# Attention's exponentials: the clip on GpSimd, both heads' sums in one VectorE instruction, six buffers

## The chip, the cores and the metric

The kernel runs on one core of one Trainium2 chip. The metric is the device time of one execution in microseconds (us). Before the change it is 1333.87 us, the median of 3 runs (1332.39 to 1336.94).

## The reference, cut to what matters

A block of a gated cross-attention model in float32: attention of 2048 rows over 1601 context rows, and then a quantised feed-forward network (FFN).

```python
# attention: x (1, 2048, 256), ctx_1024 (1, 1601, 256), 16 heads of 64
q = (lat @ Wq); k, v = split(ctx @ Wkv)
attn = einsum('bhnd,bhsd->bhns', q, k) * D ** (-0.5)
attn = jnp.clip(attn, -11.0, 11.0)
attn = jax.nn.softmax(attn, axis=-1)
out = einsum('bhns,bhsd->bhnd', attn, v)
x = x + tanh(g_xattn[0]) * (out @ Wo + bo)
# FFN: weights quantised to 4 bits by blocks of 32, activations to 16 bits
up = act_qdq(x @ lpbq_dequant(w_up).T); gate = act_qdq(x @ lpbq_dequant(w_gate).T)
...
x = x + tanh(g_ffn[0]) * (o @ lpbq_dequant(w_down).T)
```

The kernel clips the exponentials, not the scores: exp grows with its argument, so clipping exp(s) to exp(-11) and exp(11) gives the same numbers.

## The kernel before, in words

**Segments and tiles.** Attention is 32 segments (`SEGS`, `t0` from 0 to 31): 8 pairs of heads by 4 blocks of 512 query rows. A segment runs over 13 tiles (`ST`, `st` from 0 to 12) of 128 context rows, the last of 65. Each engine has its own program, written out by hand; semaphores order them, and an engine waits at the head of its own queue.

**One tile.** PE makes the scores of both heads (`scores`, L916) in PSUM, two buffers deep. ScalarE takes the exponentials of both heads into a slot of `e_buf` (L443, 128x1024). VectorE clips them in place (L662). PE multiplies them with V (`values`, L932). The softmax denominators are sums over the context, so the clipped tiles are also added into `acc`: head 0 by VectorE (`add_a`, L622), head 1 by GpSimd (L346), 128x512 each. `e_buf` has 4 slots, and an exponential waits until its slot's `values` and both sums are done.

**PE's order.** Within a segment PE runs `scores(st + 2)`, then what `segment_jobs` puts at `st`, then `values(st)`. So between the end of `scores(st)` and the start of `values(st)` lie at least four matmul groups. The jobs are projections of K and V for the next pair at 0, Q and the denominators (`den`) at 4, and the output projection (`y`) at 10. They share two PSUM banks; a bank is free once the engine that takes its result has done so.

**VectorE beside the tiles.** For the segment before, it joins the two halves of the output (`join_out`, L643), inverts the denominators in four pieces at tiles 6 and 7 (L629, from PSUM), scales the output with them at tile 8 (`scale_out`, L637, which the `y` job waits for), and adds `y` to `xacc` at tile 12 (L652).

**Other work.** In segments 25 to 27 the FFN's weights are quantised: maxima, scales and rounding on VectorE (L559, L599, L600, L604), two products a weight piece on GpSimd (L360, 128x768), two pieces a segment. In segments 30 and 31 VectorE also does the FFN's layer norm of finished rows (`ffn_norm`, L531 to L559). In segment 0 GpSimd adds the output bias to `xacc` (L351). GpSimd scales Wo with the gate once in four segments (L332). DMA issues stand on SP alone.

Of the kernel before, what the change touches and what calls it, by code (L numbers as in the profile page):

```python
# [106 lines left out]
def attention_ffn(nc, x, ctx_rows, g_xattn, g_ffn, ln_l_w, ln_l_b, ln_c_w, ln_c_b,  # L107
                  Wq, Wkv, Wo, bo, w_gate, w_up, w_down, out):
    with ExitStack() as ctx:
# [196 lines left out]
        def _(pool):  # L306
# [17 lines left out]
            def run(seg):  # L324
                t0 = seg.t0
                if t0 % NBS == 0:
                    p = t0 // NBS

                    pool.wait_ge(w_loaded[p % 2], (p // 2 + 1) * 64)
                    if t0 > NBS:  # L330
                        await_job(pool, ("y", t0 - NBS - 1, 1), seg)
                    pool.tensor_tensor(wo_g[:, p % 2, :], wo_raw[:, p % 2, :], tg[:, 0:1].to_broadcast([P, DM]),  # L332
                                       ALU.mult).then_inc(wo_scaled, 1)
                for st in range(1, ST):
                    r = rows_of(st)

                    pool.wait_ge(clip_done, seg.count(ST, st + 1))
                    if st == 1:
                        if t0 >= 2:

                            await_job(pool, ("den", t0 - 2), seg)
                        a = e_buf[:, (ST * t0) % E_BUFS, 1, :]
                    else:
                        pool.wait_ge(sum_b, seg.count(ST - 1, st - 1))
                        a = acc[0:r, t0 % 2, 1, :]
                    pool.tensor_tensor(acc[0:r, t0 % 2, 1, :], a, e_buf[0:r, (ST * t0 + st) % E_BUFS, 1, :],  # L346
                                       ALU.add).then_inc(sum_b, 1)
                    if t0 == 0 and st > ST - 9:

                        for t in range(2 * (st - ST + 8), 2 * (st - ST + 9)):  # L350
                            pool.tensor_tensor(xacc[:, t, :], xacc[:, t, :], bo_t[:, :], ALU.add).then_inc(bias_added, 1)  # L351

                    n, at = divmod(st, 6)
                    if WQ0 <= t0 < WT0 and at in (2, 5) and n < 2:

                        w = 2 * (t0 - WQ0) + (0 if at == 2 else 1)
# [160 lines left out]
        def _(dve):  # L517
# [137 lines left out]
            def run(seg):  # L655
                t0 = seg.t0
                p = t0 // NBS + 1
                for st in range(ST):
# [437 lines left out]
```

## Time and profile before

| | us |
|---|---|
| median of 3 runs (lowest, highest) | 1333.87 (1332.39, 1336.94) |
| the profiled execution | 1334.15 |
| its span | 1332.2 |
| around the span | 1.95 |
| busy: PE, VectorE, GpSimd, ScalarE | 1201.8, 1113.6, 704.4, 602.3 |

The span runs from the first to the last instruction; the profiled execution's own time is that span and what lies around it. Busy time counts an instruction from its start to its end, waits for a port inside it included. Matmuls overlap, so their starts say more than their lengths.

### The profile page before, as it was taken

The page shows a single profiled execution, that of the slowest core. Times are in us where ns is not written, and L with a number is a line of the kernel's source. Part 1 is how long each engine was busy: PE and PEld are TensorE (multiplying, and loading weights), DVE is VectorE, ACT ScalarE, POOL GpSimd, SP SyncE. Part 2 cuts the span into 40 slices and gives each one's busy share as a digit, 9 for nine tenths or more (in the row PEclk, how much of TensorE's full clock was granted, in tenths as well). Part 3 has the DMA queues.
Part 4 walks back from the last instruction along what each step waited for, and adds up shares of the span by engine and source line. Part 5 has one row for each costly group of instructions (what it writes and reads, how often), then busy time and mean ns, then how long its engine had stood idle before and what let it go on. Part 6 is the DMA issues. An engine that isn't in the chain of part 4 may idle for free.

```text
span 1332.2 us, 21513 instructions
## 1 busy us (share of the span) xinstructions
PE 1201.8 (90%) x8427; PEld 501.4 (38%) x8427; DVE 1113.6 (84%) x1432; ACT 602.3 (45%) x682; POOL 704.4 (53%) x457
## 2 busy tenths in 40 slices
PE   4999999999999999999999999999889988699118
PEld 2433333333333333333333333333223322377118
DVE  6598888888888888888888888889999998857985
ACT  2544444444444444444444444444334543158642
POOL 1685655556556555665565556566776655102400
PEclk9999999999999999999999999999999999699559
DMA  4000000000000000000000002000000000000001
GB/s 148 1 1 17 1 1 1 13 5 1 1 2 16 1 1 1 17 1 1 1 17 1 1 1 88 1 1 1 1 1 1 1 1 1 0 1 1 0 0 64
DMA packets 17107, 13.90 MB, mean 10 GB/s; under 512 B 2221, under 2 KB 16750, under 8 KB 17006
## 3 DMA queue, kind: packets, MB, share of 16 engines
q1 hardware_dynamic: 17006, 12.53, 3.0%
q8 instruction: 67, 1.10, 0.3%
q14 instruction: 34, 0.28, 0.1%
HBM read 10.43 MB, written 2.10 MB: 9 GB/s over the span
## 4 chain that ended last, share of the span: by engine, by line
PE 65%; DVE 21%; issue 7%; ACT 5%; POOL 1%; DMA 0%; POOLq 0%; SPq 0%; DVEq 0%
PE ps L932 21%; PE ps L916 20%; DVE e_buf L662 6%; PE ps L1027 6%; PE ps L890 4%; PE ps L847 4%; DVE oT L637 4%; DVE rden L629 4%; PE ps L855 4%; PE ps L864 3%; DVE acc L622 3%; ACT e_buf L443 2%; PE ps L875 2%; ACT z L498 1%; PE ps L836 1%
## 5 line engine op out<-in xcount | busy, mean ns | idle before, releaser
L346 POOL TENSOR_TENSOR acc<-acc,e_buf 128x512 f32<-128x512 f32 (+1 forms) x352 | 583.1, 1657 | 365.1 <-DVE e_buf L662 364.4
L443 ACT ACTIVATE e_buf<-ps 128x1024 f32<-128x1024 f32 (+1 forms) x416 | 426.2, 1025 | 492.3 <-PE ps L916 490.9
L662 DVE TENSOR_SCALAR e_buf<-e_buf 128x1024 f32<-128x1024 f32 (+1 forms) x416 | 472.5, 1136 | 150.4 <-ACT e_buf L443 147.2
L932 PE MATMUL ps<-e_buf,vb 64*64 64x512 f32 (+1 forms) x3328 | 473.5, 601 | 44.0 <-DVE e_buf L662 42.8
L622 DVE TENSOR_TENSOR acc<-acc,e_buf 128x512 f32<-128x512 f32 (+1 forms) x352 | 254.7, 724 | 0.0
L916 PE MATMUL ps<-qb,kb_even 64*64 64x512 f32 (+1 forms) x1664 | 234.6, 595 | 1.3 <-ACT e_buf L443 1.3
L916 PE MATMUL ps<-qb,kb_odd 64*64 64x512 f32 (+1 forms) x1664 | 232.8, 593 | 0.0
L932 PEld LDWEIGHTS ps<-e_buf,vb 64*64 64x64 f32 (+1 forms) x3328 | 118.4, 132 | 301.2 <-issue 191.8
L916 PEld LDWEIGHTS ps<-qb,kb_even 64*64 64x64 f32 (+1 forms) x1664 | 63.5, 131 | 134.3 <-issue 117.2
L916 PEld LDWEIGHTS ps<-qb,kb_odd 64*64 64x64 f32 (+1 forms) x1664 | 63.4, 131 | 132.1 <-issue 114.2
L629 DVE RECIPROCAL rden<-ps 128x128 f32<-128x128 f32 x124 | 109.0, 919 | 0.0
L346 POOL TENSOR_TENSOR acc<-e_buf 128x512 f32<-128x512 f32 x32 | 41.2, 1288 | 69.0 <-DVE e_buf L662 69.0
L1027 PE MATMUL ps<-hT,wgu 128*128 128x512 f32 x288 | 69.6, 404 | 1.8 <-DVE hT L753 1.8
L890 PE MATMUL ps<-wo_g,oT 128*128 128x256 f32 x256 | 66.6, 404 | 2.4 <-issue 2.4
L847 PE MATMUL ps<-latT,wst 128*128 128x512 f32 x128 | 65.2, 632 | 1.1 <-ACT latT L385 1.1
L890 PEld LDWEIGHTS ps<-wo_g,oT 128*128 128x128 f32 x256 | 47.4, 196 | 38.7 <-issue 32.6
L370 POOL TENSOR_SCALAR z<-z 128x1024 uint16<-128x1024 f32 x12 | 14.4, 1200 | 89.5 <-ACT z L500 89.5
L1027 PEld LDWEIGHTS ps<-hT,wgu 128*128 128x128 f32 x288 | 55.2, 193 | 15.6 <-DVE hT L753 2.2
L559 DVE TENSOR_REDUCE fst<-gt 128x2 f32<-128x1024 f32 x36 | 43.5, 1213 | 17.9 <-ACT gt L484 17.9
L637 DVE TENSOR_TENSOR oT<-oT,rden 128x512 f32<-128x512 f32 x31 | 54.8, 1767 | 0.0
L864 PEld LDWEIGHTS ps<-wst,ctxT 128*128 128x128 f32 (+1 forms) x416 | 49.4, 187 | 11.2 <-issue 11.2
L855 PE MATMUL ps<-ctxT,wst 128*128 128x512 f32 (+1 forms) x128 | 52.0, 533 | 0.0
(102 smaller groups left out, 755.4 us busy)
## 6 DMA issues: line engine op xcount, KB each, us to landing
xacc<-in_x_dram SPq DMA_DIRECT2D x4, 512.0 KB, 7.5
wst<-in_L_xattn_Wkv_dram SPq DMA_DIRECT2D x16, 128.0 KB, 2.4
out_dram<-z SPq DMA_DIRECT2D x8, 256.0 KB, 2.2
e_buf<-in_ctx_dram SPq DMA_DIRECT2D x3, 512.0 KB, 4.9
wst<-in_L_xattn_Wq_dram SPq DMA_DIRECT2D x8, 128.0 KB, 2.3
wo_raw<-in_L_xattn_Wo_dram SPq DMA_DIRECT2D x8, 128.0 KB, 3.1
z<-in_L_ffn_w_gate_dram SPq DMA_DIRECT2D x1, 768.0 KB, 5.1
z<-in_L_ffn_w_up_dram SPq DMA_DIRECT2D x1, 768.0 KB, 6.9
```

What stands on the lines that cost most here:

```text
L346: pool.tensor_tensor(acc[0:r, t0 % 2, 1, :], a, e_buf[0:r, (ST * t0 + st) % E_BUFS, 1, :], ALU.add).then_inc(sum_b, 1)
L443: nc.scalar.activation(e_buf[0:r, g % E_BUFS, :, :], sc[0:r, g % 2, :, :], ACT.Exp, scale=float(DH) ** -0.5).then_inc(exp_done, 1)
L622: dve.tensor_tensor(acc[0:r, t0 % 2, 0, :], a, e_buf[0:r, (ST * t0 + st) % E_BUFS, 0, :], ALU.add).then_inc(sum_a, 1)
L629: ins = dve.reciprocal(rden[:, c * w:(c + 1) * w], ps_m[:, bank, c * w:(c + 1) * w])
L637: dve.tensor_tensor(oT[:, t % 2, :], oT[:, t % 2, :], rden[:, :], ALU.mult).then_inc(norm_done, 1)
L662: dve.tensor_scalar(tile, tile, EXP_LO, EXP_HI, ALU.max, ALU.min).then_inc(clip_done, 1)
L847: ins = pe.matmul(bank, wst[:, at[0], 0, k, :], latT[:, k, b * NB:(b + 1) * NB], start=(k == 0), stop=(k == KT - 1))
L855: ins = pe.matmul(bank[:, 0:w], wst[:, at[0], 1, k, :], ctxT[:, k, b * NB:b * NB + w], start=(k == 0), stop=(k == KT - 1))
L890: ins = pe.matmul(bank[:, DM * m:DM * m + DM], oT[:, t % 2, n0:n0 + P], wo_g[:, p % 2, :], start=True, stop=True)
L916: ins = pe.matmul(sc[at:at + n, g % 2, h, :], kb[p % 2][rows, P * st + at:P * st + at + n], qb[rows, t0 % 2, :], start=True, stop=True)
L932: ins = pe.matmul(ps_o[DH * h:DH * h + DH, half, :], vb[rows, p % 2, st, DH * h:DH * h + DH], e_buf[rows, g % E_BUFS, h, :], start=(st == ...
L1027: ins = pe.matmul(out_ap, lhs(i), rhs(j), start=(first and n == 0), stop=(last and n == 2))
```

## The change

GpSimd now clips each tile of exponentials (both heads, in place). VectorE no longer clips; it adds both heads' sums in one 128x1024 instruction (`add_e`), and one semaphore, `summed`, stands for the two. The bias additions (four of 128x1024) and the weight products go to VectorE. `e_buf` has six slots. The product for Wo is issued after the clip of tile 6, not at the segment's head.

```diff
-E_BUFS = 4
+E_BUFS = 6
...
+                for st in range(ST):
+                    tile = e_buf[0:rows_of(st), (ST * t0 + st) % E_BUFS, :, :]
+                    pool.wait_ge(exp_done, seg.count(ST, st + 1))
+                    pool.tensor_scalar(tile, tile, EXP_LO, EXP_HI, ALU.max, ALU.min).then_inc(clip_done, 1)
+                    if st == 6 and t0 % NBS == 0:
+                        p = t0 // NBS
+                        pool.wait_ge(w_loaded[p % 2], (p // 2 + 1) * 64)
...
-                        act.wait_ge(sum_a, back.count(ST - 1, s0))
-                        act.wait_ge(sum_b, back.count(ST - 1, s0))
+                        act.wait_ge(summed, back.count(ST - 1, s0))
...
+            def add_e(seg, st):
 
                 t0, r = seg.t0, rows_of(st)
                 if st == 1:
-                    a = e_buf[:, (ST * t0) % E_BUFS, 0, :]
+                    a = e_buf[:, (ST * t0) % E_BUFS, :, :]
                 else:
-                    a = acc[0:r, t0 % 2, 0, :]
-                    dve.wait_ge(sum_a, seg.count(ST - 1, st - 1))
+                    a = acc[0:r, t0 % 2, :, :]
+                    dve.wait_ge(summed, seg.count(ST - 1, st - 1))
                 dve.wait_ge(clip_done, seg.count(ST, st + 1))
...
+                dve.tensor_tensor(acc[0:r, t0 % 2, :, :], a, e_buf[0:r, (ST * t0 + st) % E_BUFS, :, :],
+                                  ALU.add).then_inc(summed, 1)
...
-                    r, g = rows_of(st), ST * t0 + st
-                    dve.wait_ge(exp_done, seg.count(ST, st + 1))
-                    tile = e_buf[0:r, g % E_BUFS, :, :]
-                    dve.tensor_scalar(tile, tile, EXP_LO, EXP_HI, ALU.max, ALU.min).then_inc(clip_done, 1)
-                    if st >= 2:
-                        add_a(seg, st - 1)
-                    elif st == 0 and t0 >= 1:
-                        add_a(Seg(t0 - 1), ST - 1)
-                    elif st == 1 and t0 >= 1:
+                    if st >= 1:
+                        add_e(seg, st)
+                    elif t0 >= 1:
                         join_out(seg, t0 - 1)
+                    if t0 == 0 and 4 <= st < 4 + NBS:
+                        add_bias(st - 4)
...
-                        if st < 2:
-                            w_scales(w + st)
-                        if st in (7, 11):
-                            w_integers(w + st // 11)
+                        if st in (0, 6):
+                            w_scales(w + st // 6)
+                        if st in (1, 7):
+                            w_multiply(w + st // 7, 2, w_inverse, w_scaled)
+                        if st in (2, 8):
+                            w_integers(w + st // 8)
+                        if st in (3, 9):
+                            w_multiply(w + st // 9, 1, w_round, w_quant)
```

VectorE in an ordinary segment, from the sum at tile 5 to that at tile 8 (L662 is the clip, L622 the sum of head 0, L629 the inversion, L637 the scaling). Before:

```order
L662 TENSOR_SCALAR e_buf<-e_buf 128x1024
L622 TENSOR_TENSOR acc<-acc,e_buf 128x512
L629 RECIPROCAL rden<-ps 128x128 x2
L662 TENSOR_SCALAR e_buf<-e_buf 128x1024
L622 TENSOR_TENSOR acc<-acc,e_buf 128x512
L629 RECIPROCAL rden<-ps 128x128 x2
L662 TENSOR_SCALAR e_buf<-e_buf 128x1024
L622 TENSOR_TENSOR acc<-acc,e_buf 128x512
L637 TENSOR_TENSOR oT<-oT,rden 128x512
L662 TENSOR_SCALAR e_buf<-e_buf 128x1024
L622 TENSOR_TENSOR acc<-acc,e_buf 128x512
```

After, a whole segment's sums up to tile 11 (L604 is the sum of both heads, L618 the inversion, L626 the scaling):

```order
L604 TENSOR_TENSOR acc<-e_buf 128x1024
L604 TENSOR_TENSOR acc<-acc,e_buf 128x1024 x5
L618 RECIPROCAL rden<-ps 128x128 x2
L604 TENSOR_TENSOR acc<-acc,e_buf 128x1024
L618 RECIPROCAL rden<-ps 128x128 x2
L604 TENSOR_TENSOR acc<-acc,e_buf 128x1024
L626 TENSOR_TENSOR oT<-oT,rden 128x512
L604 TENSOR_TENSOR acc<-acc,e_buf 128x1024 x3
```

The clips are gone from between the sums, the inversions and the scaling; the scaling stands behind the sum of tile 8 as before behind that of tile 7.

GpSimd at the start of a segment whose number divides by four (L332 is the product for Wo, L346 the sum of head 1). Before:

```order
L332 TENSOR_TENSOR wo_g<-wo_raw,tg 128x256
L346 TENSOR_TENSOR acc<-e_buf 128x512
L346 TENSOR_TENSOR acc<-acc,e_buf 128x512 x10
L346 TENSOR_TENSOR acc<-acc,e_buf 65x512
L346 TENSOR_TENSOR acc<-e_buf 128x512
L346 TENSOR_TENSOR acc<-acc,e_buf 128x512 x10
```

After (L329 is the clip, L335 the product for Wo):

```order
L329 TENSOR_SCALAR e_buf<-e_buf 128x1024 x7
L335 TENSOR_TENSOR wo_g<-wo_raw,tg 128x256
L329 TENSOR_SCALAR e_buf<-e_buf 128x1024 x5
L329 TENSOR_SCALAR e_buf<-e_buf 65x1024
L329 TENSOR_SCALAR e_buf<-e_buf 128x1024 x12
```

The clips stand one behind another, with nothing between them but that product.

VectorE at tiles 6 to 8 of segment 25, the first with weight work (L604 is the rounding, L622 the sum). Before:

```order
L622 TENSOR_TENSOR acc<-acc,e_buf 128x512
L629 RECIPROCAL rden<-ps 128x128 x2
L662 TENSOR_SCALAR e_buf<-e_buf 128x1024
L622 TENSOR_TENSOR acc<-acc,e_buf 128x512
L629 RECIPROCAL rden<-ps 128x128 x2
L604 TENSOR_SCALAR z<-z 128x768
L662 TENSOR_SCALAR e_buf<-e_buf 128x1024
L622 TENSOR_TENSOR acc<-acc,e_buf 128x512
L637 TENSOR_TENSOR oT<-oT,rden 128x512
```

After (L534, L574, L575 are the scales of the second weight piece, L592 its first product, L604 the sum, L626 the scaling):

```order
L618 RECIPROCAL rden<-ps 128x128 x2
L534 TENSOR_REDUCE wsc<-z 128x24
L574 TENSOR_SCALAR wsc<-wsc 128x24
L575 RECIPROCAL wsc<-wsc 128x24
L604 TENSOR_TENSOR acc<-acc,e_buf 128x1024
L618 RECIPROCAL rden<-ps 128x128 x2
L592 TENSOR_TENSOR z<-z,wsc 128x768
L604 TENSOR_TENSOR acc<-acc,e_buf 128x1024
L626 TENSOR_TENSOR oT<-oT,rden 128x512
```

The scales have come from tile 1 to tile 6, and the product that GpSimd did stands ahead of the sum and the scaling at tile 8.

## Rows read from the trace of the kernel before

**Rows 1.** Page: the span of the profiled execution.

```profile
span 1332.2 us, 21513 instructions
```

**Rows 2.** Windows: stretch, us, busy time of each engine (instructions), PEclk, DMA share, GB/s.

```profile
93.00:420.00 327.00, 319.85 (x2334) 117.68 (x2333) 277.13 (x324) 148.88 (x164) 191.68 (x119) 1.00 0.02 6
...
890.00:1005.00 115.00, 102.92 (x724) 35.96 (x720) 108.23 (x123) 46.10 (x51) 82.07 (x49) 0.97 0.00 1
```

**Rows 3.** Timeline: ScalarE's L429 copies, one a segment: start us, us, instruction.

```profile
384.26 0.59 ACT L429 COPY oT<-ps 128x512 f32<-128x512 f32 x1 [0.80 <-PE ps L932]
...
418.65 0.59 ACT L429 COPY oT<-ps 128x512 f32<-128x512 f32 x1 [0.81 <-PE ps L932]
...
450.37 0.59 ACT L429 COPY oT<-ps 128x512 f32<-128x512 f32 x1 [0.81 <-PE ps L932]
...
889.41 0.59 ACT L429 COPY oT<-ps 128x512 f32<-128x512 f32 x1 [0.80 <-PE ps L932]
...
1004.36 0.59 ACT L429 COPY oT<-ps 128x512 f32<-128x512 f32 x1 [0.81 <-PE ps L932]
...
1067.76 0.59 ACT L429 COPY oT<-ps 128x512 f32<-128x512 f32 x1 [0.81 <-PE ps L932]
...
1104.26 0.59 ACT L429 COPY oT<-ps 128x512 f32<-128x512 f32 x1 [0.81 <-PE ps L932]
...
1145.80 0.59 ACT L429 COPY oT<-ps 128x512 f32<-128x512 f32 x1 [11.33 <-PE ps L932]
```

**Rows 4.** Timeline, PE in segment 10: start us, us, engine line.

```profile
405.73 1.04 PE L932 MATMUL ps<-e_buf,vb 64*64 64x512 f32 x8
...
406.59 1.04 PE L916 MATMUL ps<-qb,kb_even 64*64 64x512 f32 x8
...
408.34 1.09 PE L932 MATMUL ps<-e_buf,vb 64*64 64x512 f32 x8 [0.71 <-DVE e_buf L662]
...
411.16 1.99 PE L890 MATMUL ps<-wo_g,oT 128*128 128x256 f32 x8
```

**Rows 5.** Timeline, other engines in segment 10.

```profile
405.48 1.65 POOL L346 TENSOR_TENSOR acc<-acc,e_buf 128x512 f32<-128x512 f32 x1 [1.17 <-DVE e_buf L662]
...
405.91 1.77 DVE L637 TENSOR_TENSOR oT<-oT,rden 128x512 f32<-128x512 f32 x1
...
407.60 0.68 DVE L662 TENSOR_SCALAR e_buf<-e_buf 128x1024 f32<-128x1024 f32 x1
...
407.69 1.02 ACT L443 ACTIVATE e_buf<-ps 128x1024 f32<-128x1024 f32 x1 [0.69 <-PE ps L916]
```

**Rows 6.** Waits of PE, 93 to 1005 us: total, times, longest.

```profile
PE ps L932 <- DVE e_buf L662: 29.0, 32, 2.2
```

**Rows 7.** Groups by line: busy us, mean ns, idle before them.

```profile
L346 POOL TENSOR_TENSOR acc<-acc,e_buf 128x512 f32<-128x512 f32 (+1 forms) x352 | 583.1, 1657 | 365.1 <-DVE e_buf L662 364.4
...
L662 DVE TENSOR_SCALAR e_buf<-e_buf 128x1024 f32<-128x1024 f32 (+1 forms) x416 | 472.5, 1136 | 150.4 <-ACT e_buf L443 147.2
...
L622 DVE TENSOR_TENSOR acc<-acc,e_buf 128x512 f32<-128x512 f32 (+1 forms) x352 | 254.7, 724 | 0.0
...
L319 POOL TENSOR_SCALAR z<-xacc,lnt 128x256 f32<-128x256 f32 x12 | 6.5, 558 | 14.0 <-DVE lnt L591 14.0
```

**Rows 8.** Timeline, FFN: one-input GpSimd beside two-input VectorE.

```profile
1210.51 1.05 POOL L370 TENSOR_SCALAR z<-z 128x1024 uint16<-128x1024 f32 x1 [66.96 <-ACT z L500]
...
1242.41 1.62 POOL L370 TENSOR_SCALAR z<-z 128x1024 uint16<-128x1024 f32 x1 [1.77 <-ACT z L500]
...
1241.90 1.22 DVE L772 TENSOR_TENSOR gt<-z 128x1024 f32<-128x1024 int16 x1
...
1261.78 2.10 DVE L783 TENSOR_TENSOR gt<-z,ui 128x1024 f32<-128x1024 int16 x1
```

**Rows 9.** Timeline, VectorE at the end of segment 31.

```profile
1143.48 0.68 DVE L622 TENSOR_TENSOR acc<-acc,e_buf 65x512 f32<-65x512 f32 x1
...
1147.70 1.76 DVE L705 RECIPROCAL rden<-ps 128x256 f32<-128x256 f32 x1 [0.59 <-PE ps L875]
```

More of the change, by code:

```diff
@@ L325, in run @@
                 t0 = seg.t0
[L326 to L356, printed above, removed]
-                        blocks = wpiece[w].rearrange("p (n e) -> p n e", e=QB)
-                        by = wsc[:, w, 2 - n, :].unsqueeze(2).to_broadcast([P, WBLK, QB])
-                        pool.wait_ge((w_inverse, w_round)[n], w + 1)
-                        pool.tensor_tensor(blocks, blocks, by, ALU.mult).then_inc((w_scaled, w_quant)[n], 1)
@@ new lines, in run @@
+                for st in range(ST):
[5 more added lines that the diff above has]
+                        pool.wait_ge(w_loaded[p % 2], (p // 2 + 1) * 64)
+                        if t0 > NBS:
+                            await_job(pool, ("y", t0 - NBS - 1, 1), seg)
+                        pool.tensor_tensor(wo_g[:, p % 2, :], wo_raw[:, p % 2, :], tg[:, 0:1].to_broadcast([P, DM]),
+                                           ALU.mult).then_inc(wo_scaled, 1)
@@ L611, in w_low, with w_multiply, add_bias @@
                                   ALU.subtract).then_inc(job_taken[bank_of(key)], 1)
-            def add_a(seg, st):
+            def w_multiply(w, row, ready, done):
+                blocks = wpiece[w].rearrange("p (n e) -> p n e", e=QB)
+                dve.wait_ge(ready, w + 1)
+                dve.tensor_tensor(blocks, blocks, wsc[:, w, row, :].unsqueeze(2).to_broadcast([P, WBLK, QB]),
+                                  ALU.mult).then_inc(done, 1)
+            def add_e(seg, st):
                 t0, r = seg.t0, rows_of(st)
                 if st == 1:
-                    a = e_buf[:, (ST * t0) % E_BUFS, 0, :]
+                    a = e_buf[:, (ST * t0) % E_BUFS, :, :]
                 else:
-                    a = acc[0:r, t0 % 2, 0, :]
-                    dve.wait_ge(sum_a, seg.count(ST - 1, st - 1))
+                    a = acc[0:r, t0 % 2, :, :]
+                    dve.wait_ge(summed, seg.count(ST - 1, st - 1))
                 dve.wait_ge(clip_done, seg.count(ST, st + 1))
-                dve.tensor_tensor(acc[0:r, t0 % 2, 0, :], a, e_buf[0:r, (ST * t0 + st) % E_BUFS, 0, :],
-                                  ALU.add).then_inc(sum_a, 1)
+                dve.tensor_tensor(acc[0:r, t0 % 2, :, :], a, e_buf[0:r, (ST * t0 + st) % E_BUFS, :, :],
+                                  ALU.add).then_inc(summed, 1)
+            def add_bias(b):
+                dve.wait_ge(bias_scaled, 1)
+                dve.wait_ge(lat_pool, NT - 4)
+                rows = xacc[:, 4 * b:4 * b + 4, :]
+                dve.tensor_tensor(rows, rows, bo_t[:, :].unsqueeze(1).to_broadcast([P, 4, DM]), ALU.add).then_inc(bias_added, 1)
             def invert(seg, t, c):
@@ L649, in add_y @@
                 if seg.t0 <= 4:
-                    dve.wait_ge(bias_added, NT)
+                    dve.wait_ge(bias_added, NBS)
                 dst = xacc[:, n0:n0 + 2, :]
@@ L696, in _ @@
             end = Seg(SEGS)
-            add_a(Seg(SEGS - 1), ST - 1)
             t = SEGS - 1
@@ L871, in den_job @@
                 s = Seg(t)
-                pe.wait_ge(sum_a, s.count(ST - 1, ST - 1))
-                pe.wait_ge(sum_b, s.count(ST - 1, ST - 1))
+                pe.wait_ge(summed, s.count(ST - 1, ST - 1))
                 for h in range(2):
```

2 lines of the change are left out of this document (1 added, 1 removed).

## The prediction

> **What bounds the kernel now.** I read the page first, for the span of 1332.2 us [rows 1], then the windows. In ten segments of pure attention PE is busy 319.9 of 327 us; in the three with weight work, 102.9 of 115, and there VectorE is busy 108.2 [rows 2]. So attention is PE's, with small holes, and VectorE's where weights are quantised. The lengths of segments come from ScalarE's copies, one a segment [rows 3]: 418.65 - 384.26 = 34.39 us, and 450.37 - 418.65 = 31.72 where the K and V jobs are short. Segments 25 to 27 take 1004.36 - 889.41 = 114.95 where the same jobs would take 2 x 34.39 + 31.72 = 100.5. Segment 30 takes 36.5, segment 31 41.5.
>
> PE's starts show what one hole is. Groups of matmuls start 0.86 us apart; after the scores at 406.59, `values` should start at 407.45, and starts at 408.34, 0.89 late, waiting for the clip [rows 4]. VectorE is late with that clip because of a port: GpSimd's sum runs from 405.48 to 407.13, VectorE's scaling starts at 405.91 and takes 1.77, and the clip begins only at 407.60 [rows 5]. The waits give the count: 32, 29.0 us together [rows 6]. Segments 2 to 24 and segment 1 have one each, 24 x 0.71 = 17.0 as the profile counts it, 24 x 0.89 = 21.4 in lost start time; the rest lies in segments 25 to 27.
>
> **The change, step by step.**
>
> *The port.* VectorE's clip has a mean of 1136 ns, but takes 0.68 when nothing holds it [rows 5, 7]; the sum of head 0 takes 724 ns on average, the one on GpSimd 1657 [rows 7]. The FFN shows the pair that the change makes, one input on GpSimd and two on VectorE, 1024 columns each: GpSimd alone 1.05 us; the one issued at 1242.41 beside VectorE's 1241.90 to 1243.12 ends at 1244.03, which is 0.91 behind VectorE's end; and VectorE's own goes from 1.22 to 2.10 when it comes second [rows 8]. So they take turns. The Trainium skill says so too (SBUF — State Buffer, "Who interferes with whom"): a VectorE instruction with two SBUF inputs and a GpSimd instruction that reads SBUF exclude each other, the second fully blocks. By that rule, the trace agrees.
>
> *The clip on GpSimd.* No row of before has float32 out of GpSimd at 1024 columns. The nearest is 1.05 us with 16-bit output [rows 8]. The other end comes from 128x256 in float32, 558 ns with two per-partition scalars [rows 7]: if all of it grew with the columns it were 2.2 us, if 0.2 us of it are fixed, 1.6. I take 1.05 to 1.1, since the FFN row has the same columns and immediates as operands; I keep 1.6 for the range.
>
> *The sum of both heads.* 1.22 us, as VectorE's two-input instruction of 1024 columns [rows 8]. Nothing faster is to be had: 0.68 for 512 [rows 9] and 1.22 for 1024 make about 0.54 a 512 columns and 0.14 fixed, so 0.95 for the weight products of 768.
>
> *Is a clip in time?* From the end of `scores(st)` to the start of `values(st)` lie four groups, 4 x 0.86 = 3.44 us. ScalarE starts 0.24 behind the scores' end (407.69 against 407.45) and takes 1.02 [rows 4, 5], so the clip has 2.18 us less about 0.1 for semaphores. If the port is free it needs 1.05; if a sum has just begun, 1.22 + 0.91 = 2.13. It fits, barely, once. In a run of tiles with no job between, both take turns: a sum starts when its clip ends (+1.27), the next clip ends 0.91 behind it, 2.18 a tile against PE's 1.72. Followed from the first job-free tile of a segment, clip 3 has 1.1 us to spare, clip 4 0.6, clip 5 0.2, and then the jobs at tile 4 (Q and den, the time of three groups, 2.6 us) make it all up. The second run is helped by the inversions, which read PSUM and leave the port alone: GpSimd clips ahead while VectorE inverts. I find no clip late there. GpSimd's own load is 13 x 1.05 = 14 us and at most 12 x 1.1 of waiting, 27 of a segment's 31 to 34.
>
> *Is the scaling in time for `y`?* It waits for VectorE's queue: the sums of tiles 6, 7, 8 and four inversions. In before it ends at 407.68 and `y` starts at 411.16 [rows 4, 5], 3.5 us to spare, in a queue in which a clip and a half sum take 1.20 a tile; the whole sum takes 1.22 to 1.27 and can wait up to 0.9 for a clip. Three tiles of that cost up to 2.9 more, and 0.9 less is lost to the hole; about 1 us stays. I cost it at nothing; if this cover goes, each segment pays the excess.
>
> *Six buffers.* Sums may lag by five tiles before an exponential waits for its slot. With four slots, the waits for slots would come first where VectorE is loaded. The edit costs nothing by itself.
>
> *The product for Wo.* One GpSimd instruction behind clip 6, at most as long as a sum of 512 columns, 1.65 us [rows 5]. Clip 7's exponential comes only after the Q and den jobs and two groups, 4.3 us, so it is covered; uncovered it would be 8 x 1.65 = 13.
>
> *Bias.* Four sums of 1.22 us on VectorE in segment 0, where no inversion, scaling or join stands in its queue; they cover it, and uncovered it is 4.9 us. GpSimd loses sixteen additions that no one waits for before segment 1. Nothing either way.
>
> *Weights, segments 25 to 27.* VectorE was busy 108.2 us in 115 [rows 2]. It loses 39 clips (39 x 1.136 = 44.3) and 36 half sums (36 x 0.724 = 26.1) and gets 36 whole sums (36 x 1.25 = 45) and 12 products (12 x 0.95 = 11.4): 94.2 us of its own, to which come waits for GpSimd's 39 clips, each 0 to 0.9 us, so 94 to 129. About a third of the most, 11 us, since GpSimd usually waits for the sum and not the other way, makes 105. PE's bound is 100.5 - 3 x 0.89 = 97.8. I take 105: 10 us won; the ends are 17 won and 14 lost.
>
> *Segments 30 and 31.* Here the layer norms sit between the clips, and PE stands. After, clips pass by them on GpSimd; the norms delay only sums. In segment 31 the end is VectorE's queue. It ends its last sum at 1144.16 and inverts at 1147.70, 3.5 us later, because `values` 12 and the join come behind the last clip [rows 9]. With `values` done long before, the inversion follows the last sum by about 1.3: 2 us won. The queue itself has 26 items of 0.6 against 12 of about 1.13: 2 us less, and some port waits. I take 5 us for both segments, 2 to 9 as ends.
>
> *Sum.* 24 x 0.89 = 21.4 for ordinary segments, of which I leave 0.1 a segment (2.4) to clips that come a little late: 19. With 10 and 5 that is 34. The profiled execution took 1334.15, so 1300. The median is 1333.87, 0.3 less, which changes nothing: 1300.
>
> **The rivals.**
>
> *A. Clips come late (gain partly eaten).* The spare 0.2 us of clip 5 and the 1 us of the scaling are thin. If alternation costs 0.3 us more a tile, each segment has a hole of 0.4 to 0.8 again, 28 x 0.6 = 17 us: 1317. For it speaks that both sides stand at the margin; against it that in the second run the inversions free the port.
>
> *B. GpSimd's clip is slow, and the kernel is slower.* If float32 output takes 1.6 us, a turn of clip and sum is 1.46 + 1.27 = 2.7 against 1.72; three job-free tiles twice a segment then lose about 1 us each less the spare 1.1 and 1, so 3 to 4 us a segment. Less the 0.9 won, 2.5 x 31 = 78 us more: about 1400. The point at which it decides is a clip of about 1.3 us, where the hole is 0.9 again. The 558 ns for 256 columns speak for it, the 1.05 for 1024 against it [rows 7, 8]. The Trainium skill (GPSIMD Engine Reference, "Engine selection") speaks against the change as a whole: two-input elementwise work is about 2x slower there, one-input work roughly at line rate. By the 2x, on VectorE's 0.68, the clip would take 1.4 and we would be in B; by its one-input rule, in the main case.
>
> *C. The turns are not taken.* If clip and sum ran side by side, no clip would be late and weights would run at PE's bound: 21.4 + 17 + 9, so 1287. Rows 8 speak against it.
>
> *D. VectorE is the new bound.* It was busy 277.1 us in 327, 9.7 segments [rows 2], 28.6 each. Less 13 clips (14.8) and 12 half sums (8.7), with 12 whole sums (15.0), it has 20.1 of its own; with 0.9 for each of 13 clips 31.8, above the 30.8 left of a short segment. Then 6 short segments lose 1 us, and a lag that reaches the scaling as much again in the others: 1300 + 24 = 1324 at most. Since most waits are GpSimd's, I do not expect the full 0.9.
>
> **How the numbers follow.** Main case 0.58, 1290 to 1309; A 0.16 and D 0.06, 1310 to 1328, a few of them within 0.3% of before; B 0.14; C 0.06. Faster or slower by over 0.3% (4 us, about what can be told from no change): B's milder half (clip of 1.3) ends near 1334, so same 0.05, slower 0.11, faster 0.84. To hold 8 in 10 the range takes the main case, C, and A and D up to 1322: 1284 to 1322.
>
> **What would show it.** GpSimd clips of 1.05 us, or up to 2 when they follow a sum; sums of 1.22, or 2.1 behind a clip. Ordinary segments of 33.5 us by ScalarE's copies, with no wait of `values` for a clip. The three weight segments together about 105, the last two 73. I am wrong if a free clip takes over 1.2 us, if PE waits for GpSimd once a segment or more, or if `y` waits for the scaling.

## The result, and the profile after

| | us |
|---|---|
| before, median of 4 runs (lowest, highest) | 1333.17 (1332.39, 1336.94) |
| after, median of 4 runs (lowest, highest) | 1835.59 (1833.28, 1836.73) |
| ratio, with its 95% interval | 1.3766 (1.374, 1.3793) |

The change makes the kernel 502 us slower; the forecast was 1300 (1284 to 1322). The page of the kernel after: its span, the chain that ended last, and its three costliest groups (busy us, mean ns of one, idle time before them).

```profile
span 1831.2 us, 20320 instructions
...
POOL 79%; PE 12%; issue 3%; ACT 3%; DVE 2%; DMA 0%; POOLq 0%; SPq 0%; DVEq 0%
...
L329 POOL TENSOR_SCALAR e_buf<-e_buf 128x1024 f32<-128x1024 f32 (+1 forms) x416 | 1548.8, 3723 | 50.1 <-ACT e_buf L418 17.9
L604 DVE TENSOR_TENSOR acc<-acc,e_buf 128x1024 f32<-128x1024 f32 (+1 forms) x352 | 710.5, 2018 | 504.0 <-POOL e_buf L329 503.8
L919 PE MATMUL ps<-e_buf,vb 64*64 64x512 f32 (+1 forms) x3328 | 512.4, 640 | 401.8 <-POOL e_buf L329 400.4
```

The chain alone tells it: 79% of the span hangs on GpSimd. A clip (L329) takes 3723 ns on average where the prediction had 1.05 to 1.1 us, or 2 behind a sum. GpSimd sat idle for only 50 us ahead of 416 clips, and PE waited 400 us for them. The view of that one line shows that the length is the clip's own, with hardly a wait inside it: minimum and median are the same (shortest, median and longest in ns, then the first and the last start).

```profile
L329 POOL TENSOR_SCALAR e_buf<-e_buf x416: 3618/3622/4663, 42.7 to 1636.0; 128x1024 f32<-128x1024 f32 x128, 65x1024 f32<-65x1024 f32 x11
```

The windows, in the columns of [rows 2]:

```profile
93.00:420.00 327.00, 248.71 (x1580) 80.97 (x1580) 187.88 (x127) 101.44 (x113) 316.26 (x87) 0.93 0.01 4
890.00:1005.00 115.00, 85.46 (x560) 28.24 (x560) 67.09 (x47) 37.31 (x42) 112.62 (x31) 0.96 0.02 5
```

In 327 us GpSimd is busy 316.3; PE falls from 319.9 to 248.7. The whole time can be put together from the clips. They begin at 42.7 and the last ends at about 1639.6, 1596.9 us later: 1548.8 of clips, eight products for Wo of 0.61, and some 43 idle. Behind it lie 191.6 us, the end of attention and the FFN (before, 1332.2 less the end of the last clip at about 1141.8: 190.4). So 42.7 + 1596.9 + 191.6 is the span, and what stands ahead of the clips and behind them takes nearly as long as before. GpSimd is the kernel.

ScalarE's copies, one a segment, as in [rows 3] (here L405):

```profile
497.54 0.59 ACT L405 COPY oT<-ps 128x512 f32<-128x512 f32 x1 [2.88 <-PE ps L919]
...
546.60 0.59 ACT L405 COPY oT<-ps 128x512 f32<-128x512 f32 x1 [2.79 <-PE ps L919]
```

This segment takes 49.1 us, against 34.4; segments 1 to 24 take 47.9 to 52.5, on average 49.9. Thirteen clips that start 3.70 us apart make 48.1. The timeline inside it:

```profile
507.46 1.09 PE L919 MATMUL ps<-e_buf,vb 64*64 64x512 f32 x8 [1.66 <-POOL e_buf L329]
507.51 2.09 DVE L604 TENSOR_TENSOR acc<-acc,e_buf 128x1024 f32<-128x1024 f32 x1 [3.58 <-POOL e_buf L329]
...
511.16 1.09 PE L919 MATMUL ps<-e_buf,vb 64*64 64x512 f32 x8 [1.75 <-POOL e_buf L329]
511.21 2.09 DVE L604 TENSOR_TENSOR acc<-acc,e_buf 128x1024 f32<-128x1024 f32 x1 [1.61 <-POOL e_buf L329]
```

`values` and the sum start together, each time a clip ends, 3.70 us apart. The sum then takes 2.09 us beside the next clip, not 1.22, and still ends before that clip does.

### The profile page after: what moved, and what is told of

Read it like the earlier page. It is cut to its first block, busy times and chain, and to the rows that moved or that the text cites. A ratio compares the mean times of both kernels' runs of the same rounds, so it can differ in the third digit from the quotient of the medians.

```text
span 1831.2 us, 20320 instructions
## 1 busy us (share of the span) xinstructions
PE 1334.6 (73%) x8427; PEld 501.1 (27%) x8427; DVE 1147.3 (63%) x1032; ACT 603.8 (33%) x682; POOL 1585.7 (87%) x461
## 4 chain that ended last, share of the span: by engine, by line
POOL 79%; PE 12%; issue 3%; ACT 3%; DVE 2%; DMA 0%; POOLq 0%; SPq 0%; DVEq 0%
POOL e_buf L329 78%; PE ps L1014 4%; PE ps L919 2%; PE ps L843 2%; PE ps L903 2%; PE ps L852 1%; ACT z L473 1%; ACT e_buf L418 1%; ACT z L475 1%; DVE gt L771 1%; ACT up L459 1%; POOL ui L349 0%; DVE fst L534 0%; PE ps L877 0%; DMA e_buf<-in_ctx_dram 0%
## 5 line engine op out<-in xcount | busy, mean ns | idle before, releaser
L329 POOL TENSOR_SCALAR e_buf<-e_buf 128x1024 f32<-128x1024 f32 (+1 forms) x416 | 1548.8, 3723 | 50.1 <-ACT e_buf L418 17.9
L604 DVE TENSOR_TENSOR acc<-acc,e_buf 128x1024 f32<-128x1024 f32 (+1 forms) x352 | 710.5, 2018 | 504.0 <-POOL e_buf L329 503.8
L919 PE MATMUL ps<-e_buf,vb 64*64 64x512 f32 (+1 forms) x3328 | 512.4, 640 | 401.8 <-POOL e_buf L329 400.4
L418 ACT ACTIVATE e_buf<-ps 128x1024 f32<-128x1024 f32 (+1 forms) x416 | 425.9, 1024 | 882.4 <-PE ps L903 882.4
L919 PEld LDWEIGHTS ps<-e_buf,vb 64*64 64x64 f32 (+1 forms) x3328 | 99.7, 136 | 746.9 <-POOL e_buf L329 609.3
L903 PE MATMUL ps<-qb,kb_even 64*64 64x512 f32 (+1 forms) x1664 | 246.3, 627 | 1.3 <-ACT e_buf L418 1.3
L903 PE MATMUL ps<-qb,kb_odd 64*64 64x512 f32 (+1 forms) x1664 | 246.9, 628 | 0.0
L604 DVE TENSOR_TENSOR acc<-e_buf 128x1024 f32<-128x1024 f32 x32 | 40.1, 1253 | 117.1 <-POOL e_buf L329 117.1
L618 DVE RECIPROCAL rden<-ps 128x128 f32<-128x128 f32 x124 | 108.9, 917 | 0.0
L346 POOL TENSOR_SCALAR z<-z 128x1024 uint16<-128x1024 f32 x12 | 14.4, 1198 | 92.0 <-ACT z L475 92.0
L843 PE MATMUL ps<-ctxT,wst 128*128 128x512 f32 (+1 forms) x128 | 75.9, 738 | 0.0
L877 PE MATMUL ps<-wo_g,oT 128*128 128x256 f32 x256 | 67.2, 407 | 6.6 <-issue 6.5
L877 PEld LDWEIGHTS ps<-wo_g,oT 128*128 128x128 f32 x256 | 47.6, 196 | 41.2 <-issue 34.9
L534 DVE TENSOR_REDUCE fst<-gt 128x2 f32<-128x1024 f32 x36 | 43.6, 1215 | 18.7 <-ACT gt L459 18.7
L852 PE MATMUL ps<-wst,ctxT 128*128 128x128 f32 (+1 forms) x416 | 55.2, 287 | 0.0
L405 ACT COPY oT<-ps 128x512 f32<-128x512 f32 x32 | 18.8, 586 | 110.3 <-PE ps L919 110.3
```

The lines of the kernel that those rows point to most:

```text
L329: pool.tensor_scalar(tile, tile, EXP_LO, EXP_HI, ALU.max, ALU.min).then_inc(clip_done, 1)
L418: nc.scalar.activation(e_buf[0:r, g % E_BUFS, :, :], sc[0:r, g % 2, :, :], ACT.Exp, scale=float(DH) ** -0.5).then_inc(exp_done, 1)
L534: return dve.tensor_reduce(dst, src, AX_X, ALU.max, apply_absolute_value=True)
L604: dve.tensor_tensor(acc[0:r, t0 % 2, :, :], a, e_buf[0:r, (ST * t0 + st) % E_BUFS, :, :], ALU.add).then_inc(summed, 1)
L618: ins = dve.reciprocal(rden[:, c * w:(c + 1) * w], ps_m[:, bank, c * w:(c + 1) * w])
L843: ins = pe.matmul(bank[:, 0:w], wst[:, at[0], 1, k, :], ctxT[:, k, b * NB:b * NB + w], start=(k == 0), stop=(k == KT - 1))
```

## The experiments

Two theories to start with. **O, the operations**: a clip (max, then min) is a slow pair of operations on GpSimd, whatever stands around it; the FFN row from which I took 1.05 us multiplies twice. **The rivals**: the float32 output, the clip in place, or the port shared with VectorE makes it slow. Behind that stand two more questions: is the rest of the prediction (1300 with a clip of about 1.05) sound, and is the hole in the kernel before due to the port?

### The forms of the instruction, by themselves

> Leaves out the whole block: it writes zeros and only times forms of one-input GpSimd instructions, each four times alone (no VectorE work beside them), and at the end clips and products beside VectorE sums. In the changed kernel a clip takes 3.62 us at the least, in the FFN the product of two immediates with 16-bit output takes 1.05. Theory O (the operations): max and min are slow on GpSimd whatever the output: clip 3.6 out of place and in place, product in float32 about 1.05, one max alone somewhere between, a clip of 512 columns about 1.9. Theory F (float32 output): the product with float32 output is 3.6 too and only the 16-bit one 1.05. Theory I (in place): out-of-place clip about 1.05, in-place clip and in-place product 3.6. Theory P (the port, VectorE beside it): the clip alone takes 1.05 in all forms and only the last group 3.6.

Groups by line and form. Each form ran four times, in order, with VectorE idle (but for two fills of memory at the start, during L64). Only L94 ran beside VectorE's two-input sums, and of its four the last had none left beside it. L64 is mult, mult (two multiplications in one instruction, each by its own number); L66 the clip into another tensor and L68 in place; L70 mult, mult in place; L72 max alone; L76 mult alone; L78 mult, add; L80 add, subtract; L82 mult, mult to 16 bits; L84 and L86 the clip on 512 and 256 columns.

```profile
L94 POOL TENSOR_SCALAR c<-b 128x1024 f32<-128x1024 f32 x4 | 16.1, 4015 | 0.3
L80 POOL TENSOR_SCALAR c<-b 128x1024 f32<-128x1024 f32 x4 | 14.5, 3632 | 0.3
L66 POOL TENSOR_SCALAR c<-b 128x1024 f32<-128x1024 f32 x4 | 14.5, 3621 | 0.3
L68 POOL TENSOR_SCALAR b<-b 128x1024 f32<-128x1024 f32 x4 | 14.5, 3621 | 0.3
L76 POOL TENSOR_SCALAR c<-b 128x1024 f32<-128x1024 f32 x4 | 11.1, 2770 | 0.3
L72 POOL TENSOR_SCALAR c<-b 128x1024 f32<-128x1024 f32 x4 | 11.1, 2766 | 0.3
...
L84 POOL TENSOR_SCALAR c<-b 128x512 f32<-128x512 f32 x4 | 7.7, 1916 | 0.3
...
L86 POOL TENSOR_SCALAR c<-b 128x256 f32<-128x256 f32 x4 | 4.2, 1061 | 0.3
L64 POOL TENSOR_SCALAR c<-b 128x1024 f32<-128x1024 f32 x4 | 4.2, 1044 | 0.3
L78 POOL TENSOR_SCALAR c<-b 128x1024 f32<-128x1024 f32 x4 | 4.2, 1044 | 0.3
L82 POOL TENSOR_SCALAR u<-b 128x1024 uint16<-128x1024 f32 x4 | 4.2, 1044 | 0.3
L70 POOL TENSOR_SCALAR b<-b 128x1024 f32<-128x1024 f32 x4 | 4.2, 1044 | 0.3
```

The clip takes 3621 ns alone, in place or not. Mult, mult takes 1044 to float32, to 16 bits, and in place: output type and place cost nothing. The port costs a little: 4015 on average, and 4410 at the most, against 3621. O holds. It is also finer than I had put it. Two operations are slow or fast as a pair: add, subtract is as slow as the clip, mult, add as fast as mult, mult. And a single operation, a multiplication too, takes 2770, longer than two multiplications in one instruction.

### The kernel after with a cheap operation in the clip's place

```diff
-pool.tensor_scalar(tile, tile, EXP_LO, EXP_HI, ALU.max, ALU.min).then_inc(clip_done, 1)
+pool.tensor_scalar(tile, tile, 1.0, 1.0, ALU.mult, ALU.mult).then_inc(clip_done, 1)
```

> The changed kernel with GpSimd's clip made a product with 1.0 twice, same place, shapes, waits and types: the clipping of the exponentials is left out. Theory O: GpSimd's instruction falls from 3.62 to about 1.05 us and the kernel comes to what was forecast, near 1300 us. Theories F, I and P: still 3.6 us and about 1835 us.

1298.53 us (2 runs), 0.9737 of before (0.9699 to 0.9775). The groups that were 3723 and 2018 ns, and the copies of two segments:

```profile
L329 POOL TENSOR_SCALAR e_buf<-e_buf 128x1024 f32<-128x1024 f32 (+1 forms) x416 | 538.4, 1297 | 520.8 <-ACT e_buf L418 519.9
L604 DVE TENSOR_TENSOR acc<-acc,e_buf 128x1024 f32<-128x1024 f32 (+1 forms) x352 | 518.8, 1474 | 192.9 <-POOL e_buf L329 188.5
...
376.90 0.58 ACT L405 COPY oT<-ps 128x512 f32<-128x512 f32 x1 [0.81 <-PE ps L919]
...
410.35 0.58 ACT L405 COPY oT<-ps 128x512 f32<-128x512 f32 x1 [0.81 <-PE ps L919]
```

Only the operations differ, and 537 us go. With the price that the prediction gave the clip, its own sum comes out: segments of 33.44 us, 103.5 for segments 25 to 27, and 1298.5 against 1300.

One sign that the prediction named is there all the same: `y` waits for the scaling. In ordinary segments 1.3 us are left between the end of the scaling and the start of `y`; in segments 25, 26, 27 and 31 PE stands idle for 1.3, 1.3, 3.0 and 6.4 us, and `y` starts 0.1 us behind the scaling. The profile names no releaser for these waits; the times do. Segment 27 (L626 is the scaling, L877 `y`):

```profile
962.30 1.52 DVE L626 TENSOR_TENSOR oT<-oT,rden 128x512 f32<-128x512 f32 x1
963.92 1.97 PE L877 MATMUL ps<-wo_g,oT 128*128 128x256 f32 x8 [3.03 <-issue]
```

The three waits of 25 to 27 make 5.7 us, which is just what these segments take above PE's bound of 97.8.

### The clip back on VectorE, the rest of the change kept

GpSimd keeps only the product for Wo; the clip stands in VectorE's queue ahead of each sum, as in the kernel before, and the sums are whole.

```diff
+                    tile = e_buf[0:rows_of(st), g % E_BUFS, :, :]
+                    dve.tensor_scalar(tile, tile, EXP_LO, EXP_HI, ALU.max, ALU.min).then_inc(clip_done, 1)
+                    if st >= 2:
+                        add_e(seg, st - 1)
```

> The changed kernel with the clip back on VectorE, all else of the change kept (both heads' sum in one VectorE instruction, bias and weight products on VectorE, six buffers); GpSimd has only the Wo products. If GpSimd's clip is the whole loss, and the port the cause of before's hole at tile 9: clip 0.68, sum 1.22, no waits for the port, ordinary segments 33.5 us, about 1300. If instead VectorE's queue is the bound without GpSimd's help (0.6 + 1.25 a tile is more than PE's 1.72), clips come late in runs of tiles without jobs and it is 1340 to 1370.

1325.44 us (6 runs), 0.9938 (0.9919 to 0.9957), between my two forecasts and neither of them. The parts of the change other than the clip's engine are worth 8 us by themselves, nearly all in segments 25 to 27 (107.4 us, from 115.0); moving the clip costs the other 510. But segments stay at 34.37 and 31.70, although GpSimd does nothing there. VectorE's timeline of one segment:

```profile
403.28 1.76 DVE L614 RECIPROCAL rden<-ps 128x128 f32<-128x128 f32 x2
...
405.50 1.21 DVE L600 TENSOR_TENSOR acc<-acc,e_buf 128x1024 f32<-128x1024 f32 x1
406.63 0.69 DVE L622 TENSOR_TENSOR oT<-oT,rden 128x512 f32<-128x512 f32 x1
407.24 0.69 DVE L647 TENSOR_SCALAR e_buf<-e_buf 128x1024 f32<-128x1024 f32 x1
```

The scaling takes 0.69, no turn is lost, and yet the clip of tile 9 ends late: here two inversions, a clip, a whole sum and a scaling stand ahead of it. So the queue on VectorE is enough to make such a hole. Whether it made the one in the kernel before was open again; the last experiment answers it.

### Six buffers alone

The kernel before with `E_BUFS = 6`.

> The kernel before with six exponential buffers and nothing else changed. If the buffers never bind in before (one wait of an exponential for a slot in its profile), 1333 within 0.3%. If VectorE's or GpSimd's lag reaches the exponentials in the weight segments, up to 5 us faster.

1332.94 us (10 runs), 0.9998 (0.9986 to 1.0011): nothing, as costed.

### One operation: only the lower clip

```diff
+pool.tensor_scalar(tile, tile, EXP_LO, None, ALU.max).then_inc(clip_done, 1)
```

> The changed kernel with only the lower bound clipped (one operation, max): the upper clip is left out. By the forms run GpSimd then takes 2.77 us a tile where the full clip takes 3.62. If the loss is GpSimd's length and nothing else, each tile costs GpSimd 2.85 with the gap between two, in segments where PE needs 2.6 a tile on average: about 1835 - 416 x 0.85 = 1482 us. If the loss came from the port that the clip takes from VectorE's sums, half of it or more would stay: over 1600.

1447.57 us (1 run), where I had 1482. The clips still add up to the time: 42.6 ahead of the first, 1151.4 for 416 of them, some 60 idle and in Wo products, and 192 behind. I had taken 0.85 us off each clip, the difference when each runs alone. In the kernel their means differ by more, 3.72 against 2.80, and 416 x 0.93 = 386 us is the fall from 1835.6. Most of these clips take as long as they do alone:

```profile
L329 POOL TENSOR_SCALAR e_buf<-e_buf x416: 2756/2763/3739, 42.6 to 1251.1; 128x1024 f32<-128x1024 f32 x128, 65x1024 f32<-65x1024 f32 x11
```

### The clip on VectorE with the sums moved out of the loaded tiles

No sums at tiles 6 to 8, where the inversions and the scaling stand; they are caught up at tiles 9 to 12.

```diff
+                    late = {6: (), 7: (), 8: (), 9: (5, 6), 10: (7, 8), 11: (9, 10), 12: (11,)} if t0 < SEGS - 1 else {}
...
+                        for s in late.get(st, (st - 1,)):
+                            add_e(seg, s)
```

> The clip on VectorE as in the run of that name, and in tiles 6 to 8 VectorE does no sums: inversions and scaling follow the clips, and the sums are caught up at tiles 9 to 12 (two at 9, 10 and 11), which six buffers allow. The run with the clip on VectorE kept a hole of 0.9 us a segment though no port wait was left, with clips 8 and 9 behind inversions, sums and scaling. If the queue makes the hole: gone, segments of 33.45 and 30.8 us, about 1325 - 29 x 0.9 = 1299. If the hole has another cause (an exponential late, the scores), it stays and the time is 1325.

1313.96 us (4 runs), 0.9859 (0.9841 to 0.9878). Long segments fall to 33.44, so in this kernel the hole was the queue. Short ones stop at 31.46, for a reason that the timeline names: `values` of tile 0 now waits for the join, which stands behind the late sum of the segment before.

```profile
410.45 1.09 PE L924 MATMUL ps<-e_buf,vb 64*64 64x512 f32 x8 [0.62 <-DVE oT L628]
```

Segments 25 to 31 became about 8 us longer than in the run with whole sums in their places; there the sums that are caught up meet the weight work and the layer norms. So 1314 and not 1299.

### The same with the second weight piece at tiles 10 to 12

> As the run with late sums, and the second weight piece of segments 25 to 27 is handled at tiles 10 to 12, behind the output projection, not at 6 to 9. In the run with the clip on VectorE these three took 107.4 us against a bound of 97.7. If VectorE's queue at tiles 6 to 9 is what binds there: 3 to 6 us less than the run with late sums, about 1295. If its total load binds, no difference.

1318.17 us (4 runs), 0.9891 (0.9871 to 0.9912): worse by 4, a miss. Segments 25 to 27 took 109.8 us, against 108.3, and segment 28 took 36.1, against 33.3. The piece now meets the sums that are caught up at the same tiles, and its lag reaches the next segment; that reading is argued, not shown.

### One inversion a tile, at tiles 5 to 8

The clip on VectorE, sums in their places, and the four inversions spread where the kernel before does two at tile 6 and two at tile 7.

```diff
-                        if st == (4 if last else 6) + c // 2:
+                        if st == (4 + c // 2 if last else 5 + c):
```

> The clip on VectorE as in the run of that name, with the four inversions one a tile at tiles 5 to 8 and the sums in place. If it is the burst of two inversions that makes clips late, the hole goes and it comes to 1299. If it is the load between the denominators and tile 9 (the same instructions in any order but for the sums), clip 9 stays as late as before: 1325 within 0.3%.

1343.29 us (4 runs), 1.0073 (1.0056 to 1.0091): the only rearrangement that lost against before, and outside both forecasts. Segments grow from 34.37 to 34.95. The first inversion waits for its denominators, in front of everything else. VectorE then works without a pause up to the clip of tile 9, and PE waits for that clip.

```profile
403.50 0.96 DVE L614 RECIPROCAL rden<-ps 128x128 f32<-128x128 f32 x1 [1.70 <-PE ps L865]
...
413.47 1.09 PE L922 MATMUL ps<-e_buf,vb 64*64 64x512 f32 x8 [1.27 <-DVE e_buf L647]
```

### Late sums in segments 1 to 24 alone, and the join first

```diff
-...if t0 < SEGS - 1 else {}
+...if t0 < WQ0 else {}
...
-                    elif st == 0 and t0 >= 1:
-                        add_e(Seg(t0 - 1), ST - 1)
                     elif st == 1 and t0 >= 1:
                         join_out(seg, t0 - 1)
+                        add_e(Seg(t0 - 1), ST - 1)
```

> The kernel after with the clip back on VectorE, with no sums at tiles 6 to 8 (caught up at tiles 9 to 12) in segments 1 to 24 alone, and with the join of two output halves issued ahead of the late sum of the segment before, not behind it. The whole computation is kept. Queue theory (where the hole stands is decided by what lies ahead of a clip in VectorE's queue): the run without the sums at tiles 6 to 8 took 1314; its long segments were at 33.44 us, its short ones at 31.46 with a wait of 0.62 us for the join, eight of them, about 5 us to win; its segments 25 to 31 were about 8 us longer than with the sums in their places. So 1314 - 5 - 8 = 1301. Port theory (the hole comes from GpSimd and VectorE taking turns): no change against the run with the clip on VectorE and the sums in place, 1325. If the joins' gain fails, 1306.

1304.95 us (4 runs), 0.9784 (0.9753 to 0.9814): the fastest of the kernels that do all of the work, 28 us below before. Segments 1 to 24 are 33.44 and 30.77, as in the run with the cheap operation, with GpSimd idle but for the Wo products. The join was the short segments' wait. Six segments have it, not eight, which makes 4 us; segments 25 to 31 are within 1 us of the run with whole sums in their places.

### GpSimd clips one head only

```diff
+                    tile = tile[:, 1, :]
                     pool.tensor_scalar(tile, tile, EXP_LO, EXP_HI, ALU.max, ALU.min).then_inc(clip_done, 1)
```

> The kernel after, with GpSimd clipping head 1 alone (128x512); head 0's exponentials are left unclipped, so half of the clip is left out. By the run of forms such a clip takes 1.92 us on GpSimd alone, and 13 of them 25 us of a segment's 31 to 34. Length theory (the clip's length alone makes the loss): PE has 3.44 us from the end of a tile's scores to its values, less 1.26 for ScalarE, so 2.18 us for the clip; 1.92 fits when GpSimd starts at once, and a hole comes where a sum holds it up: 1298 to 1330. Port theory (every clip on GpSimd beside a sum costs a turn, as I had it): clip and sum 1.92 + 1.22 = 3.1 a tile against 1.72, about 1400. The three points for the dose are then 1.04 us a clip with 1298, 2.8 with 1448, 3.7 with 1835.

1311.51 us (2 runs), 0.9833 (0.9792 to 0.9874), and segments of 33.94 and 31.85. The length theory holds; the turns do not cost what I gave them.

```profile
L330 POOL TENSOR_SCALAR e_buf<-e_buf 128x512 f32<-128x512 f32 (+1 forms) x416 | 839.7, 2019 | 236.7 <-ACT e_buf L419 214.0
```

Four points now show what a clip's length is worth (mean in the kernel, us, and time; the second clips half of the columns):

```
mean of one   time       what GpSimd does to a tile
1.30          1298.5     mult, mult, 1024 columns
2.02          1311.5     clip, 512 columns
2.80          1447.6     max alone, 1024 columns
3.72          1835.6     clip, 1024 columns
```

Up to about 2 us the length costs little: 13 us for 416 x 0.72 = 300 us of work. The 13 is a net: ordinary segments lose 0.5 and 1.1 us, and segments 25 to 27, with half of the columns, take 100.1 in place of 103.5. From 2.80 to 3.72 each added microsecond costs one: 388 us for 416 x 0.93 = 386. No run lies between 2.02 and 2.80. An estimate from these numbers puts the bend near 2.5 us: the line through the last two points comes down to 1312 at 2.47, and 13 clips fill the average segment of 32.8 us at 2.52.

### Bias and weight products on VectorE, alone

The kernel before with that part of the change and nothing else.

> The kernel before, with one part of the change alone: the bias additions and the weight products on VectorE, in the order of the kernel after; clips, sums and slots as before. The whole computation is kept. My sum took the bias for nothing, and the products for 12 x 0.95 us on VectorE, hidden in the weight segments. VectorE was busy 108.2 us of 115 there and gets 11.4 more, so if VectorE is the bound the three segments take 120 to 126 and the kernel 1338 to 1345. If what set them was the order and the waits for GpSimd's products, they fall to about the 107.5 that they take with the clip on VectorE and whole sums, and the kernel takes 1326. The other segments stay at 34.39 and 31.72.

1333.04 us (median of 10 runs; one at 1360.61 is left out of the ratio), 0.999 (0.9975 to 1.0004). Neither of my two numbers: segments 25 to 27 take 112.5 us instead of 115.0, segments 1 to 24 stay, and the first copy comes 1.3 us later, less than that time moves between other traces (with six buffers alone it comes 1.8 earlier). In 890 to 1005 us VectorE is busy 112.5 of 115 us, 4.3 more than before [rows 2]. Its twelve products take 19.8 us there, 1.65 each and not 0.95; against that its clips fall from 1232 to about 1000 ns on average and its sums of head 0 from 879 to 679. So the products brought waits of their own, and the other instructions lost some, with less for GpSimd to do beside them.

### One wait on GpSimd, in the kernel before

GpSimd's sum of tile 8 waits for the clip of tile 9, and so leaves VectorE alone while it scales.

```diff
-                    pool.wait_ge(clip_done, seg.count(ST, st + 1))
+                    pool.wait_ge(clip_done, seg.count(ST, st + 2 if st == 8 else st + 1))
```

> The kernel before with one edit: GpSimd's sum of tile 8 waits for the clip of tile 9 and not only for its own, so that GpSimd does nothing while VectorE scales the output of the segment before. The whole computation is kept. In the trace of before that sum runs from 405.48 to 407.13, the scaling takes 1.77 us and the clip of tile 9 begins 1.1 us later than it would behind a scaling of about 0.7. Port theory (in the kernel before the hole of 0.89 us is due to that turn, as the prediction had it): the scaling takes 0.7 us, the wait of PE for the clip of tile 9 goes, segments take 33.5 and 31.7 or less, and the kernel about 1333 - 24 x 0.89 = 1312. Queue theory (the hole comes from what VectorE has to do between tiles 6 and 9, turns or not, as the run with the clip on VectorE and whole sums suggested): segments stay at 34.39 and 31.72, 1333. A hole may come back smaller at tile 10 or 11, if the late sums of GpSimd hold those clips up: 1318 to 1325.

1311.09 us (4 runs), 0.9831 (0.9814 to 0.9847), from one number in one line. The scaling (minimum, median, longest, ns), first in the kernel before, then here:

```profile
L637 DVE TENSOR_TENSOR oT<-oT,rden x31: 1755/1768/1775, 101.7 to 1122.1; 128x512 f32<-128x512 f32 x31
```

```profile
L637 DVE TENSOR_TENSOR oT<-oT,rden x31: 673/683/1757, 101.5 to 1098.9; 128x512 f32<-128x512 f32 x31
```

PE's waits for the clip, in the view of [rows 6], fall from 29.0 us in 32 to:

```profile
PE ps L932 <- DVE e_buf L662: 8.7, 7, 1.3
```

Segments 2 to 24 take 33.44 and 30.77. The sum of tile 8 had been released by the clip of tile 8, just ahead of the scaling, in every segment: a turn of 1.09 us at the one place without slack. Segments 1 to 24 win 22.6 us; of the others, 25 to 27 win 2.1 and segment 28 loses 2.7. Three late sums follow one another on GpSimd behind it, and VectorE's clips there take 1.76 us; those have slack. So in the kernel before the hole was the port; with whole sums on VectorE it was the queue. Both fill the same slack.

## Why the prediction was wrong

*What bounds the kernel, and the port.* Right. The hole of 0.89 us a segment and its cause are shown by the last experiment: the forecast for removing it was 21.4 us, measured 22.6 in the same 24 segments and 22 in the whole.

*The clip on GpSimd: the step that failed.* "I take 1.05 to 1.1, since the FFN row has the same columns and immediates as operands." That row [rows 8] is a product with two immediates. I asked whether float32 output or columns could change its price, and never whether max and min cost what multiplications cost. They cost 3.45 times as much. My upper bound, 2.2 us, came from a row of 128x256 that multiplies and adds as well [rows 7], so no bound of mine held the operations either. There was no row with max or min on GpSimd: that is a price not shown by the trace, and the range had to say so. One row of before did warn that the operations matter. A single multiplication of 128x256 takes 928 ns, where the multiplication and addition of the same shape take 558 [rows 7]:

```profile
L313 POOL TENSOR_SCALAR bo_t<-bo_t,tg x1: 928/928/928, 14.0 to 14.0; 128x256 f32<-128x256 f32 x1
```

What the clip costs on VectorE, 0.68 us, was a row of the right operations on the wrong engine.

*The Trainium skill.* By GPSIMD Engine Reference, "Engine selection", one-input work runs roughly at line rate on GpSimd. The runs come near that for mult, mult and mult, add (1044 ns for 1024 columns) and not for this clip, which takes 5.3 times VectorE's 0.68. Its other rule, two-input work about twice as slow, holds for a two-input addition (2337 ns against VectorE's 1.22 us). It was the nearest thing to a warning, and the 1.4 us that I worked out from it for the clip was too low as well.

*The sum.* Except for that term its total was right, as the run with mult, mult shows:

```
                         predicted   with mult, mult
ordinary segment         33.5        33.44
segments 25 to 27        105         103.5
segments 30 and 31       73          74.5
total                    1300        1298.5
```

The sum alone takes 1.22 us (1223 ns on average in the best kernel). The Wo product, the bias and the six buffers cost nothing that can be seen.

That the total agrees to 1.5 us is in part luck, because some terms were off and cancelled. The 2.4 us left for late clips were not needed. Segments 25 to 27 cost what they do through the waits of `y` for the scaling, which I had put at nothing; the port waits that I had added count only as far as they make the scaling late. And of the 5 us for the last two segments little comes: from ScalarE's copy that ends segment 29 to the first inversion behind segment 31 it is 79.1 us, against 79.9. The cover of 1 us that I found for `y` in ordinary segments was right (1.3).

Rivals A, C and D did not come in that run: PE waits 0.6 us in all for a clip, and the longest sum takes 2.10 us, so turns are taken.

*Rival B.* That a slow clip makes the kernel slower was named and had a chance of 0.14. Its reason, the float32 output, was wrong (1044 ns with either output), and both its numbers were off. Its clip was 1.6 us and is 3.62. And its price was too high for what it assumed: a clip with a mean of 2.02 us gave 1311, not 1400, and the point from which it decides is far above the 1.3 us that I gave. I had added 1.27 for the sum to each clip, as if the two never overlapped; instead the load of GpSimd is what counts, 13 clips against a segment's length. At 3.7 us a clip that load is 48.1 us against 33, and 32 segments of that make most of the 500.

*Turns.* I took them for whole: one engine done, then the other. The trace of after says otherwise (below).

## What to carry to other kernels

Price an instruction by a row with the same operations on the same engine, not only the same shape, types and operands; where there is none, measure that one instruction before moving 416 of them. Then compare the engine's load per segment (13 x its length) with the segment before reasoning about single deadlines. And where two engines take turns at a port, look at which instruction releases the one that gets in the way: one wait moved by a tile gave 22 us, two thirds of what the whole change was after. Last, when a total agrees, still hold its terms against the trace one by one: here the agreement hid waits of `y` of 12 us.

## What the runs showed of the hardware

- On GpSimd the pair of operations of a one-input float32 instruction sets its time. Per 128x1024: mult, mult and mult, add 1044 ns; max, min 3621 and add, subtract 3632; a single max, min or mult 2765 to 2770. A two-input addition takes 2337. The clip grows with columns: 1061, 1916, 3621 for 256, 512, 1024. Why a single multiplication is slower than a pair is not explained by anything here.
- One multiplication of 128x256 on GpSimd takes 928 ns in the kernel before, the multiplication and addition of that shape 558.
- A slow GpSimd instruction does not keep VectorE out for its whole length. A two-input sum that starts with a 3.62-us clip takes 2.09 us in place of 1.22, so it is held up for 0.87 us and ends about 1.6 us before the clip does. The Trainium skill (SBUF — State Buffer, "Who interferes with whom") says that the two exclude each other until the one is done; these rows do not agree with it. The other way round nearly the whole sum counts: a clip that starts 0.05 us behind a sum of 1.23 takes 4.66, which is 1.04 more.

```profile
502.70 1.23 DVE L604 TENSOR_TENSOR acc<-e_buf 128x1024 f32<-128x1024 f32 x1 [3.45 <-POOL e_buf L329]
502.75 4.66 POOL L329 TENSOR_SCALAR e_buf<-e_buf 128x1024 f32<-128x1024 f32 x1
...
507.49 3.62 POOL L329 TENSOR_SCALAR e_buf<-e_buf 128x1024 f32<-128x1024 f32 x1
507.51 2.09 DVE L604 TENSOR_TENSOR acc<-acc,e_buf 128x1024 f32<-128x1024 f32 x1 [3.58 <-POOL e_buf L329]
```

- How long such a sum is held up goes with the columns of the GpSimd instruction more than with its length. The sum takes up to 2.10 us beside the product of 1.04 us, 1.98 beside max alone (2.76) and 2.09 beside the clip (3.62), all of 1024 columns, but at most 1.67 beside the clip of 512 columns (1.92). What the two engines share in that time is not shown.
